# The last image's key-value product behind its last convolution, input remainders on two engines, two early loads (a two-layer attention kernel on one core)

## The reference, cut to what matters

```python
qkv = jnp.einsum('oc,bchw->bohw', w_qkv, x)                 # 768 channels
qkv_ms = jnp.concatenate([qkv, _aggreg(qkv, w_dw, w_pw)], axis=1)   # 5x5 depthwise, then 8x8 in groups
# per head: q = relu(..), k = relu(..), v1 = v with a row of ones
vk = jnp.einsum('bhdn,bhen->bhde', v1, k)
out = jnp.einsum('bhde,bhen->bhdn', vk, q)
out = out[:, :, :-1] / (out[:, :, -1:] + EPS_ATT)
out = jnp.einsum('oc,bchw->bohw', w_proj, out)
mean = jnp.mean(out, axis=(0, 2, 3), keepdims=True)         # over the batch: needs all images
var = jnp.var(out, axis=(0, 2, 3), keepdims=True)
return (out - mean) * jax.lax.rsqrt(var + EPS_BN) * gamma + beta + residual
```

## Time and profile before

| what | value |
|---|---|
| time, median of 3 runs | 2250.73 us (2247.62 to 2252.7) |
| the profiled execution | 2251.85 us, of which the span is 2250.1 us |
| PE busy | 2059.1 us, 92% of the span |
| DVE busy | 1423.8 us, 63% |
| ACT busy | 867.5 us, 39% |
| POOL busy | 646.4 us, 29% |
| mean granted TensorE clock | 0.964 of full speed |

### The profile page before, as it was taken

How to read it: one execution, slowest core, us unless ns; L and a number is a source line. 1 busy time by engine, 2 the same in 40 slices (tenths; PEclk the granted TensorE clock), 3 DMA queues, 4 the chain that set the end, 5 groups by cost and what they waited for, 6 DMA issues and landing times. The chain is left out here.

```text
span 2250.1 us, 33698 instructions
## 1 busy us (share of the span) xinstructions
PE 2059.1 (92%) x13448; PEld 1517.5 (67%) x13448; DVE 1423.8 (63%) x2052; ACT 867.5 (39%) x1841; POOL 646.4 (29%) x511
## 2 busy tenths in 40 slices
PE   8999999999897999999999999999999999999810
PEld 7888898888774666666666666766766666666500
DVE  6667776677248765948667575684857659480452
ACT  5444544444443423423433342343334234234142
POOL 1223312231324422522522242252243226221000
PEclk9999999999998999999999999999999999999855
DMA  3220122210677756764865776586486667647588
GB/s 124 85 85 17 69 85 85 85 74 12 232 268 267 250 199 239 261 225 172 288 230 203 266 265 210 194 292 216 167 303 237 209 238 252 228 172 263 237 340 373
DMA packets 144475, 450.91 MB, mean 200 GB/s; under 512 B 7744, under 2 KB 106688, under 8 KB 120000
## 3 DMA queue, kind: packets, MB, share of 16 engines
q1 hardware_dynamic: 143168, 429.89, 53.6%
q10 hardware_dynamic: 1152, 18.87, 2.0%
HBM read 273.95 MB, written 174.78 MB: 199 GB/s over the span
## 5 line engine op out<-in xcount | busy, mean ns | idle before, releaser
L791 PE MATMUL cv<-work,wc 128*64 128x288 f32 x4608 | 622.3, 415 | 15.9 <-issue 12.0
L1153 POOL TENSOR_TENSOR wc<-taps 128x512 f32<-128x512 f32 x288 | 366.3, 1299 | 499.4 <-PE cv L791 492.0
L791 PEld LDWEIGHTS cv<-work,wc 128*64 128x64 f32 x4608 | 308.3, 137 | 258.9 <-issue 51.5
L1233 DVE SCALAR_TENSOR_TENSOR spun<-work,spun 128x1152 f32<-128x1152 f32 x240 | 379.0, 1584 | 0.0
L1227 DVE STREAM_SHUFFLE spun<-work 128x1152 f32<-128x1152 f32 x240 | 347.9, 1456 | 0.1
L1015 ACT ACTIVATE work<-cv 128x288 f32<-128x288 f32 x384 | 157.6, 410 | 475.3 <-PE cv L791 473.6
L770 PE MATMUL pj<-x1hi,w1hi 128*128 128x288 f32 x768 | 237.3, 309 | 29.2 <-issue 24.3
L993 ACT COPY work<-pj 128x288 f32<-128x288 f32 x384 | 154.1, 401 | 232.4 <-PE pj L772 232.4
L772 PE MATMUL pj<-x1hi,w1lo 128*128 128x288 f32 x768 | 230.2, 300 | 0.0
L771 PE MATMUL pj<-x1lo,w1hi 128*128 128x288 f32 x768 | 229.0, 298 | 0.0
L420 POOL TENSOR_TENSOR qs<-qs,qrc 128x512 f32<-128x512 f32 x72 | 75.2, 1049 | 402.1 <-DVE qrc L474 402.1
(11 more groups left out here) (128 smaller groups left out, 3406.0 us busy)
## 6 DMA issues: line engine op xcount, KB each, us to landing
work<-scratch_padded SPq DMA_DIRECT2D x48, 1306.0 KB, 6.9
scratch_padded<-work SPq DMA_DIRECT2D x48, 1300.0 KB, 6.2
work<-scratch_padded SPq DMA_DIRECT2D x48, 1299.5 KB, 9.9
scratch_phases<-work SPq DMA_DIRECT2D x96, 576.0 KB, 4.6
work<-scratch_phases SPq DMA_DIRECT2D x64, 576.0 KB, 5.4
x<-scratch_x SPq DMA_DIRECT2D x9, 2304.0 KB, 11.2
scratch_x<-xs SPq DMA_DIRECT2D x8, 2304.0 KB, 6.9
q<-scratch_phases SPq DMA_DIRECT2D x32, 576.0 KB, 5.5
```

Source lines behind the costliest of these rows:

```text
L791: mm = nc.tensor.matmul(cv[64 * b:64 * b + 64, j % 2, :PLANE], wc[:, 2 * j + b, dy].rearrange("p c o -> p (c o)"), window, start=(dy == 0) ...
L1153: op = nc.gpsimd.tensor_tensor(wc[:, blocks, dy], taps[:, u % 2, blocks, 0:DIM].rearrange("p g (c o) -> p g c o", o=1).to_broadcast([P, HB ...
L1233: nc.vector.scalar_tensor_tensor(out=spun[:, t % 2], in0=kc[:, piece], scalar=1.0, in1=spun[:, t % 2], op0=ALU.mult, op1=ALU.mult, accum_o ...
```

## The change

Product 3 of the last image is no longer shared out between the chunks of unit 5, but runs in one piece behind them, on PE and on ACT. Pieces 2 and 3 of the remainder `x1lo` go from POOL to DVE, into the turns of product 3, and `xlo_ready` becomes two semaphores, one for pieces 0 and 1 and one for 2 and 3. The sum of the keys moves out of the end of `spin` into a function `total`, which runs ahead of the turns. In SP's last instructions of `phase_l1` the `x1` loads of the fourth and fifth image of `phase_out` are added; the `y` load of the fifth stays in `phase_out`. For this `xb` now lies at a fixed address over buffers of `phase_l1` (`w1hi`, `w1lo`, `taps`, `wc`, `spun`), so `wproj` and `spun` change places.

```diff
@@ tensor; the same two lines move likewise in scalar @@
-                        if u == 5 and i == last_image:
-                            product(i, 3, shares(AG, 0, 8)[j])
...
+                    if u == 5 and i == last_image:
+                        product(i, 3, range(AG))
@@ sync, end of phase_l1 @@
             for n, (y, x, loaded) in enumerate(early):
-                sp.dma_start(y, dram["y"][n]).then_inc(loaded, 16)
-                if x is not None:
-                    sp.dma_start(x, dram["x1"][n]).then_inc(loaded, 16)
+                if n < len(early) - 1:
+                    sp.dma_start(y, dram["y"][n]).then_inc(loaded, 16)
+                sp.dma_start(x, dram["x1"][n]).then_inc(loaded, 16)
@@ gpsimd @@
                 if i != last_image:
                     low(i + 1, [0, 1])
-                weights(i, 5, [0])
-                if i != last_image:
-                    low(i + 1, [2, 3])
-                weights(i, 5, [1])
+                weights(i, 5)
@@ vector @@
+            def total(i, p):
+                u = PRODUCTS[p][0] + PARTS.index(1)
+                for h in range(2):
+                    dve.wait_ge(lay_done[u % 2][h], laid_at(i, u))
+                wait_count(dve, dsel_ready, 4 * (i - 1) + p + 1)
+                nc.vector.tensor_reduce(vkd[:, p // 2, DIM:DIM + 1], kva[:, 0], AX.X, ALU.add)
...
                 if share[-1] == 15:
-                    wait_count(dve, dsel_ready, 4 * (i - 1) + p + 1)
-                    nc.vector.tensor_reduce(vkd[:, p // 2, DIM:DIM + 1], kc, AX.X, ALU.add)
                     dve.wait_ge(spun_summed, first + 16)
...
+                total(i, 1)
                 spin(i, 1, range(0, 6))
...
+                if i != last_image:
+                    total(i, 3)
                 if prev:
                     statistics(i - 1, Y_CHUNKS[3])
                 if i != last_image:
-                    spin(i, 3, range(0, 16))
+                    spin(i, 3, range(0, 3))
+                    low(i + 1, [2])
+                    spin(i, 3, range(3, 4))
+                    low(i + 1, [3])
+                    spin(i, 3, range(4, 16))
@@ phase_out, sync @@
+                sp.dma_start(y, dram["y"][order[k]]).then_inc(loaded, 16)
                 if k > len(early):
-                    sp.dma_start(y, dram["y"][order[k]]).then_inc(loaded, 16)
-                sp.dma_start(x, dram["x1"][order[k]]).then_inc(loaded, 16)
+                    sp.dma_start(x, dram["x1"][order[k]]).then_inc(loaded, 16)
```

More of the change, by code:

```diff
@@ L543, in phase_l1 @@
         wlo = sb("w1lo", [P, CT, NU, P], F32R)
-        wproj = sb("wproj", [P, 4, C])
         taps = sb("taps", [P, 2, NB, DIM + KROWS * NG])
         wc = sb("wc", [P, NB, KROWS, DIM, NG])
+        spun = sb("spun", [P, 2, SPIN])
+        wproj = sb("wproj", [P, 4, C])
         ident = sb("ident1", [P, P])
@@ L564, in phase_l1 @@
         rlo = sb("rlo", [P, 2, CHUNK], F32R)
-        spun = sb("spun", [P, 2, SPIN])
         sums = sb("sums", [P, 2, DIM])
@@ L586, in phase_l1 @@
         rep_in = [sem(f"l1_rep_in{r}") for r in range(3)]
-        w_split, w_rest, xhi_ready, xlo_ready = sem("l1_w_split"), sem("l1_w_rest"), sem("l1_xhi_ready"), sem("l1_xlo_ready")
+        w_split, w_rest, xhi_ready = sem("l1_w_split"), sem("l1_w_rest"), sem("l1_xhi_ready")
+        xlo_front, xlo_back = sem("l1_xlo_front"), sem("l1_xlo_back")
         lay_stored, lay_done = ((lay_stored0, lay_stored1), (lay_stored2, lay_stored3)), ((lay_done0, lay_done1), (lay_done2, lay_done3))
@@ L1206, in _, with low @@
             nc.vector.tensor_tensor(wlo[:, :, 0:2], wqkv[:, :, 0:2], whi[:, :, 0:2].bitcast(F32), ALU.subtract).then_inc(w_split, 1)
[L1208 to L1211, removed]
+            def low(i, parts):
+                for s in parts:
+                    dve.wait_ge(xhi_ready, 4 * i + s + 1)
+                    nc.vector.tensor_tensor(x_part(xlo, s), x_part(x1 if i else x1_first, s), x_part(xhi, s).bitcast(F32),
+                                            ALU.subtract).then_inc(xlo_front if s < 2 else xlo_back, 1)
+            low(0, range(4))
             dve.wait_ge(w_rest, 1)
             nc.vector.tensor_tensor(wlo[:, :, 2:], wqkv[:, :, 2:], whi[:, :, 2:].bitcast(F32), ALU.subtract).then_inc(w_rest, 1)
+            def total(i, p):
[4 more added lines that the diff above has]
+                nc.vector.tensor_reduce(vkd[:, p // 2, DIM:DIM + 1], kva[:, 0], AX.X, ALU.add)
             def spin(i, p, share):
@@ L1219, in spin @@
                 if share[0] == 0:
-                    for u in (PRODUCTS[p][0], PRODUCTS[p][0] + 1):
-                        for h in range(2):
-                            dve.wait_ge(lay_done[u % 2][h], laid_at(i, u))
+                    for h in range(2):
+                        dve.wait_ge(lay_done[(PRODUCTS[p][0] + 1) % 2][h], laid_at(i, PRODUCTS[p][0] + 1))
                 def turn(t):
@@ L1308, in sb @@
             return ctx.enter_context(nc.sbuf_tensor(name, shape, F32))
-        xb = sb("xb", [P, 2, CT, HW])
+        sb("early_x", [P, 2, CT, HW])
         gb = sb("gb", [P, 2, CT])
@@ L1318, in phase_out @@
         sh = sb("sh", [P, CT])
-        g_in, stat, root, load0, load4, scaled, summed, store0, store1, store2, store3, store4 = (
+        g_in, stat, root, load0, scaled, summed, store0, store1, store2, store3, store4 = (
             sem(f"out_{n}") for n in
-            "g_in stat root load0 load4 scaled summed store0 store1 store2 store3 store4".split())
-        y_third, _, load3 = early[2]
-        buffers = ((q[:, 2:4, :], x1[:], load0), *early[:2], (y_third, xb[:, 0], load3), (q[:, 0:2, :], xb[:, 1], load4))
+            "g_in stat root load0 scaled summed store0 store1 store2 store3 store4".split())
+        buffers = ((q[:, 2:4, :], x1[:], load0), *early)
         store = (store0, store1, store2, store3, store4)
@@ L1420, in build @@
         parts = cut(work, *[(CT, HW)] * 4)
+        xb = nc.alloc_sbuf_tensor_at("xb", [P, 2, CT, HW], F32, offset=-(-nc.sbuf_base // 32) * 32)
         early = ((parts[0], parts[1], sem("out_load1")), (parts[2], parts[3], sem("out_load2")),
-                 (y_third[:], None, sem("out_load3")))
+                 (y_third[:], xb[:, 0], sem("out_load3")), (q[:, 0:2, :], xb[:, 1], sem("out_load4")))
         phase_l1(nc, dram, sem, bnst, q, x1, xhi, xlo, work, early, x_again, ahead, x_stored)
```

4 lines of the change are left out of this document (2 added, 2 removed).

## The result

The changed kernel takes 2213.36 us (median of 4 runs, 2210.98 to 2215.66) against 2250.84 us for the kernel before (4 runs), a ratio of 0.9831 [0.9819, 0.9843]. That is 37.5 us less; the forecast was 31.1 us less, and 2213 lies in its range. The profiled execution took 2214.18 us with a span of 2212.4 us and a mean granted clock of 0.970.

The account below looks back on a forecast made before the run. PE was taken as the bound, its waits and lowered clock as winnable. 12.6 + 6.5 + 5.2 + 3.8 + 3.0 = 31.1 us off 2251.85 gave 2220.8, or 2219.6 against the median; forecast 2220 us, range 2207 to 2235.

Parts of the forecast that it names:

- What bounds the kernel: Whole kernel: PE, busy 2059.1 of 2250.1 us; winnable in the long middle are PE's waits, then its lowered clock.
- Remainders on DVE: Projection of the next image's unit 0, images 1 to 6: two PE waits removed, 2.1 us net each, 12.6 us.
- no waits left: Rival, chance 0.2: pieces 2 and 3 on DVE meet no busy POOL; 3.9 us per image in six images, 2209.
- The clock: Behind the projection waits, images 2 to 6: all five dips of PE's granted clock gone, 6.5 us; bounds 0 and 6.5.
- Image 0: First image: POOL, unit 4's weights and PE move 2.5 us ahead, two waits at L770 go; 5.2 us together.
- The product behind the last convolution: Last image, unit 5: denominators start 2.8 us earlier, plus 1 us by a higher clock; 3.8 us, bounds -5 and 7.
- Two early loads: Two x1 loads moved from phase_out into idle DMA time before it: 3.0 us of 11.4 come back; bounds 1 and 6.
- the move changes nothing: Rival, chance 0.03: last pieces arrive as late as before; only image 0's reduction and the end gain, 9 us, 2242.

## Why the prediction was right, and where its sizes were off

**What bounds the kernel:** right. All that was won in the middle was PE's waiting time and the clock behind it.

**Remainders on DVE:** the mechanism held, and so did the layout that gave it. The wait left at chunk 6 was put at 1.3 us and measured 0.92 (1.1 by start times); the new one at L838 was put at 0.5 and measured 0.2. Both are of the kind foreseen, and piece 3 ended 7.5 us behind the start of piece 2, where 7.7 had been laid out. So the steady gain was 2.7 instead of 2.1 us, 16.3 instead of 12.6 in six images. DVE and POOL did take turns: pieces of 2.2 us, not 1.35. This is what kept the rival "no waits left" from coming true, and the Trainium skill's rule ("SBUF — State Buffer", section "Who interferes with whom") agrees with it. The lack of slack at `vkd` is shown from both sides, by the reduction put back (a wait of 2.52 us) and by the two pieces together (2.54).

**The clock:** 6.5 us predicted, 6.5 found, all five dips gone. That both remaining waits are short was the reason given. The runs bear it out as far as they go: it did not fall behind 0.9 us, and fell in all or in half of the steady images behind 2.5 us. The support drawn from image 1 was weak: with the old waits put back, the clock fell in image 1 as well. What decides it is not shown, so that exactly all five dips would go was in part luck.

**Image 0:** right in kind, its size not settled; 5.2 predicted, 7.4 in the pair of traces. Its long wait shrank by 2.3 us (2.5 foreseen) and its two waits at L770, 2.5 us together (2.7 foreseen), went whole. The rest I had not counted: the wait for ACT behind the long one fell from 3.8 to 2.9 us, and the lower clock behind it lasted about half as long, some 1.7 us. But these two need not be effects of the change. The kernels with product 3 between the chunks and with the two loads in `phase_out` have the same code here as the changed one, and in their traces the wait for ACT is 4.3 and 3.9 us, and the stretch from the start of the long wait to chunk 6 of image 1 takes 224.87 and 221.09 us, where the changed kernel took 223.33. By these, image 0 gave 5.9 and 9.6 us. The foreseen 5.2 is not refuted by that.

**The product behind the last convolution:** right, if somewhat low: 3.8 predicted (2.8 for the start of the denominators and 1 for the clock behind it), 3.8 and 1.2 in the traces before and after, 3.4 and 0.5 in those of the experiment, and 5.6 by its medians. The releaser changed from the load to ACT, as foreseen, and the denominators start 13.5 us behind the start of the last chunk (13 foreseen). The product took 9.3 us alone, from 2042.9 to 2052.2 in the trace, where I put 10. The gain by the clock did not come where I put it. The first 16 matmuls of the denominators took 2.79 us as before; the next 16 took 1.50 instead of 2.79 us, but a wait of 2.75 instead of 1.46 us followed them. The 1.2 us were won behind that.

**Two early loads:** 3.0 predicted, 3.5 in the traces, 4.1 by the experiment. The first store leaves 14.61 us behind `phase_out`'s start, to the hundredth as before.

In this pair of traces no term was too large: 16.3, 6.5, 7.4, 5.0 and 3.5 are 38.7, less the 1.0 us of the later entry, against the 31.1 foreseen. The steady images account for 3.7 us of the difference and are the surest of these.

Three slips of the working moved nothing in the sum. The turn that starts at 1293.46 is DVE's fifth and not its fourth, since two turns go ahead of the first multiply-add. Eight chunks of 1.5 us from 2059.5 on end at 2071.5, not 2071.2. And the rival "the move changes nothing" was priced at 2242 us, which is 9 us faster, while its chance was counted as "no change".

## What to carry to other kernels

When work is moved to another engine to remove a wait, count that engine's own chain to its next consumer, and look there for something to take out at the same time: here the moved pieces were worth 30 us, and 27 of them were lost again when the reduction went back. Then try how the pieces are shared out and at which step of a loop they stand, since one step later for one piece cost 28.6 us here, and a third piece on the first engine won another 6.3. Loads moved into an idle stretch ahead of a saturated one gave back only what had stood in the way once the saturation began, 3.8 of 11.4 us. And where a stretch of identical code differs by up to 4 us between traces, as image 0 did, a gain read from one trace of each kernel is no better than that.

## What the runs showed of the hardware

- A remainder piece of 128x1152 on DVE took 1.35 us with POOL idle and 2.21 to 2.22 us while POOL wrote weights of 128x512. A multiply-add took 1.34 us alone, 2.17 when it met those weights at their start, and beside a piece on POOL 2.3 to 2.4 us and, at one place of each steady image before the change, 3.33.
- The granted clock fell in six images of six behind a wait of 2.52 us, and in three of six behind one of 2.54 us at the same place in the program. Behind the waits of 1.75 and 1.89 us it stayed up in image 1 of the kernel before and fell there with the pieces put back in their old place. With all pieces ahead of the weights on POOL it stayed up in one image of seven behind a wait of 3.45 us. The length of the wait alone doesn't decide it; what else does, no run here tells.
- A dip cost 1.3 us in the kernel before, 1.6 us with the two pieces together (190.04 - 188.42) and 1.7 us with all pieces on POOL ahead of the weights (190.76 - 189.07). So a wait that brings it on costs more than its length: with the reduction put back, 2.3 us more of waiting made an image 3.96 us longer.
